# Gate loads from two queues, and seven sums ahead of the magnitudes on ScalarE

## The reference

```python
# x (64, 64, 1024), cond (64, 128); wk (8, 64, 64), bias_k (8, 64)
h = gelu(cond @ W0 + b0); h = gelu(h @ W1 + b1)
att = softmax(h @ W2 + b2)                       # (64, 8)
agg_w = einsum('bk,koi->boi', att, wk)           # a 64x64 matrix for each b
y = einsum('boi,bih->boh', agg_w, x) + (att @ bias_k)[:, :, None]

def bitlinear(x, w):                             # ternary weights
    scale = mean(abs(w))
    q = round(clip(w / (scale + 1e-5), -1, 1))
    return x @ (q * scale).T

out = x + bitlinear(bitlinear(y, w_gate) * bitlinear(y, w_up), w_down)
# w_gate, w_up (2752, 1024), w_down (1024, 2752)
```

## Time and profile before

| | us |
|---|---|
| median of 3 runs | 1855.11 (1854.92 to 1855.19) |
| the profiled execution | 1855.28, with a span of 1853.5 |
| busy: TensorE, VectorE, ScalarE, GpSimd | 1797.1, 955.6, 440.6, 132.6 |
| TensorE's first matmul starts | 6.18 |
| first convolution matmul starts | 25.56 |
| GpSimd's first scaling starts | 47.34 |
| second quantised tile starts | 62.96 |

### The profile page before, as it was taken

One profiled execution on the slowest core, in us unless ns is written; L12 is line 12 of the kernel. 1 busy time (PEld: TensorE's weight loads), 2 busy tenths in 40 slices (PEclk: granted clock), 3 DMA queues, 4 the chain that ended last, 5 costly groups with the idle time before them and its releaser, 6 DMA issues.

```text
span 1853.5 us, 29483 instructions
## 1 busy us (share of the span) xinstructions
PE 1797.1 (97%) x12151; PEld 1189.7 (64%) x12151; DVE 955.6 (52%) x1529; ACT 440.6 (24%) x712; POOL 132.6 (7%) x73
## 2 busy tenths in 40 slices
PE   5698999999999999999999999999999999999999
PEld 3344454444547895488846896488955888468854
DVE  5989961177533555245642556245652455435520
ACT  4667440112111222022211222112220222112110
POOL 0864500000000000000000000000000000000000
PEclk9799999999999999999999999999999999999999
DMA  8536410041101312022110321012120222012100
GB/s 298 171 127 247 131 52 29 32 165 70 66 29 50 108 51 77 29 100 67 61 56 32 115 70 66 29 53 106 51 77 30 106 77 73 30 38 80 51 18 29
DMA packets 47980, 145.74 MB, mean 79 GB/s; under 512 B 5552, under 2 KB 5872, under 8 KB 47856
## 3 DMA queue, kind: packets, MB, share of 16 engines
q1 hardware_dynamic: 47856, 143.88, 22.2%
HBM read 117.45 MB, written 26.41 MB: 78 GB/s over the span
## 4 chain that ended last, share of the span: by engine, by line
PE 91%; DVE 4%; ACT 2%; issue 2%; POOL 1%; DMA 0%; SPq 0%; DVEq 0%; ACTq 0%; POOLq 0%
PE ps L544 49%; PE ps L727 42%; DVE msk L1190 1%; ACT g_r L882 1%; POOL ys L516 1%; DVE msk L1182 1%; PE ps L626 0%; DVE aT L237 0%; ACT wgT L911 0%; POOL ab L527 0%; DVE wsum L1061 0%; DVE ys L1109 0%; ACT wuT L911 0%; DMA inter<-in_L_cond_b_dram 0%; POOL bbc L527 0%
## 5 line engine op out<-in xcount | busy, mean ns | idle before, releaser
L727 PE MATMUL ps<-yp,wgT 128*128 128x256 f16 x3528 | 773.4, 273 | 0.3 <-issue 0.2
L727 PE MATMUL ps<-wuT,wgT 128*128 128x256 f16 x3528 | 773.4, 273 | 0.0
L544 PE MATMUL ps<-wdT,inter 128*128 128x512 fp8e4 x2688 | 593.3, 379 | 0.0
L544 PEld LDWEIGHTS ps<-wdT,inter 128*128 128x128 f16 x2688 | 262.6, 98 | 314.4
L727 PEld LDWEIGHTS ps<-yp,wgT 128*128 128x128 fp8e4 x3528 | 345.3, 98 | 45.8 <-issue 5.4
L727 PEld LDWEIGHTS ps<-wuT,wgT 128*128 128x128 fp8e4 x3528 | 345.2, 98 | 40.8
L1240 DVE SCALAR_TENSOR_TENSOR xr<-ps,osc,xr 128x512 f32<-128x512 f32 x64 | 48.0, 750 | 406.0 <-PE ps L544 406.0
L544 PE MATMUL ps<-yp,wuT 128*128 128x512 f16 x672 | 152.9, 384 | 0.0
L544 PE MATMUL ps<-yp,wgT 128*128 128x512 f16 x672 | 150.5, 382 | 1.1 <-ACT wgT L911 1.1
L1001 ACT COPY raw<-ps 128x512 f32<-128x512 f32 (+1 forms) x66 | 37.3, 566 | 392.0 <-PE ps L727 392.0
L1425 DVE TENSOR_TENSOR wuT<-ps,msk 128x512 f32<-128x512 f32 (+1 forms) x66 | 44.0, 667 | 137.0 <-PE ps L727 136.2
(11 more groups left out here) (192 smaller groups left out, 1339.8 us busy)
## 6 DMA issues: line engine op xcount, KB each, us to landing
wgT<-wcomb SPq DMA_DIRECT2D x60, 896.0 KB, 4.8
xa<-in_x_dram SPq DMA_DIRECT2D x8, 2048.0 KB, 10.2
out_dram<-xr SPq DMA_DIRECT2D x64, 256.0 KB, 2.0
wdT<-in_L_ffn_w_up_dram SPq DMA_DIRECT2D x10, 512.0 KB, 4.3
wcomb<-raw SPq DMA_DIRECT2D x11, 448.0 KB, 2.5
ys<-in_L_ffn_w_down_dram SPq DMA_DIRECT2D x9, 512.0 KB, 4.0
wcomb<-msk SPq DMA_DIRECT2D x10, 448.0 KB, 2.4
xr<-in_L_ffn_w_down_dram SPq DMA_DIRECT2D x8, 512.0 KB, 4.5
```

The lines of the kernel that those rows point to most:

```text
L544: return nc.tensor.matmul(o, l, r, start=start, stop=stop)
L727: last = nc.tensor.matmul(out, w, operand(i, OPERAND[what])[:, k, :], start=(start and h + k + i == 0), stop=(k == KQ - 1 and i == 1), ski ...
```

## The change

Three edits. Gate loads with an odd number are no longer issued by SyncE but by ScalarE, all eleven ahead of its first Gelu. ScalarE's list has seven gate sums first, and then eight pairs of a magnitude and a sum, with the eight casts of y behind them. Gate tile 21 is summed by ScalarE and no longer by VectorE. SyncE's small inputs and x keep their place among the remaining gate loads.

```diff
-    SUM_DVE = (0, 1, 7, 10, 17, 21)
+    SUM_DVE = (0, 1, 7, 10, 17)
...
-                sp.dma_start(raw(e), tiles[n][0]).then_inc(s_raw[s], 16)
+                if e >= NG or e % 2 == 0:
+                    sp.dma_start(raw(e), tiles[n][0]).then_inc(s_raw[s], 16)
...
+            for e in range(1, NG, 2):
+                nc.scalar.dma_start(raw(e), tiles[loads[e][0]][0]).then_inc(s_raw[loads[e][3]], 16)
             act.wait_ge(s_pe, 2)
             nc.scalar.activation(h1, ps[1][:, 0:B], ACT.Gelu, bias=b0_sb).then_inc(s_ca, 1)
...
-            for k, n in enumerate((4, 5, 6, 8, 9, 11, 12, 13)):
+            for n in (4, 5, 6, 8, 9, 11, 12):
                 raw_sum(n)
+            for k, n in enumerate((13, 14, 15, 16, 18, 19, 20, 21)):
                 magnitudes(0, k)
-            for n, tiles_y in ((14, ()), (15, ()), (16, (0, 1)), (18, (2, 3)), (19, ()), (20, (4, 5, 6, 7))):
                 raw_sum(n)
-                for k in tiles_y:
-                    hi_y(0, k)
+            for k in range(KH):
+                hi_y(0, k)
             copy_T(0)
...
             for k in range(4):
                 split_y(0, k)
-            raw_sum(21)
             partition_sums(0, NG)
```

## The result

| | before | after |
|---|---|---|
| median of 5 runs, us | 1855.19 (1854.92 to 1856.83) | 1864.11 (1862.42 to 1864.83) |
| ratio | | 1.0044, 95% interval 1.0032 to 1.0055 |
| profiled execution, its span | 1855.28, 1853.5 | 1864.74, 1862.9 |

The changed kernel is 8.9 us slower. The forecast was 1861.9, range 1855.5 to 1867.

A forecast was written before the change was run, and what follows sets the result against it. The prediction took the first 60 us to be a chain of waits that TensorE depends on; +6.8 us for the conditioning weight and 0 for the rest gave 1862.1, less 0.17 for the median: 1861.9 us, range 1855.5 to 1867.

The forecast's parts named there:

- The main term: Conditioning weight, queues alternating packet by packet: lands at 22.0 us, aggregation needs it at 15.20, +6.8 us; chance 0.55.
- 418 GB/s: DMA drain rate assumed for the queued bytes, taken from large packets at 16 to 18 us.
- 20 ns each: Extra DMA engine time per small packet; 113 packets up to the conditioning weight make 2.3 us.
- the bias, x, the Gelu: Second-layer bias at 14.6 us, x at 27.0, Gelu possible at 8.1: each delay hidden behind other waits.
- Tile 12: Before the first magnitude: lands at 33.3 us, summed at 34.4, hidden by 0.8 us against 35.2.
- VectorE's sum: Removing VectorE's 1.20 us sum: threshold up to 1.2 us earlier, but value 0 since the chain runs through GpSimd.
- TensorE's clock: Shifted half-clock stretch at convolution or aggregation: minus 2 to up to plus 5 us.
- Rival 1: Small inputs slip through, but tile 12 delays the first magnitude: plus 5, 1860 us; chance 0.15.
- Rival 2: ScalarE's loads fill only what DMA engines leave free: net minus 1 to plus 2, 1855 us; chance 0.20.
- rival 3: Aggregation also at half clock, or ScalarE's full queue holds up SyncE's issues: 6.8 + 5, 1867 us; chance 0.10.

The follow-up runs named there:

- experiment 6: Changed kernel, but SyncE issues all small inputs ahead of gate tile 0; 1862.9 us, ratio 1.0039 to the kernel before.
- experiment 2: Kernel before with only the odd gate loads moved to ScalarE's queue, ScalarE's list and VectorE's sums as before; 1862.89 us, ratio 1.0043.
- experiments 3: Changed kernel, but ScalarE issues its eleven loads behind the Exp instead of ahead of the first Gelu; 1858.03 us, ratio 1.0015 to the kernel before.
- experiment 5: Kernel before with one edit: ScalarE issues the odd gate loads behind its Exp, old list kept; 1853.62 us, ratio 0.9989.
- experiment 8: Kernel before with SyncE's small inputs ahead of gate tile 0, SCD = 5, tile 21 summed by ScalarE, three sums before the first magnitude; 1851.25 us, ratio 0.9974.
- experiment 1: Changed kernel's ScalarE list and tile 21 sum on ScalarE, but all gate loads in SyncE's queue; 1857.25 us, ratio 1.0009 to the kernel before.

## Why the prediction was right

**The main term.** The forecast put +6.8 us on the conditioning weight, by packets taken in turn. The turns are in the trace (520 to 519), and the aggregation came 8.1 us later. The mechanism was right and the term 1.3 us too small. The gap is there from the start and doesn't grow: the first bias held TensorE until 10.67 instead of "about 9", the second layer's until 16.14 instead of 14.6, and the conditioning weight landed at 23.17 instead of 22.0. The sum let the queues drain at 418 GB/s from the first moment. The stretches view has the engines slower in the first three microseconds, and again from 12 to 14 us (the last two columns are their share and GB/s):

```profile
1.00:2.00 1.00, 0.00 (x0) 0.00 (x0) 0.00 (x0) 0.00 (x0) 0.94 (x6) 1.00 0.37 53
2.00:3.00 1.00, 0.00 (x0) 0.00 (x0) 0.00 (x0) 0.00 (x0) 0.49 (x2) 1.00 0.65 176
...
12.00:14.00 2.00, 0.01 (x1) 0.00 (x0) 0.00 (x0) 0.31 (x1) 0.00 (x0) 1.00 0.85 311
```
```profile
2.00:20.00 18.00, 2.44 (x9) 1.72 (x9) 1.39 (x8) 4.74 (x9) 0.49 (x2) 1.00 0.99 365
```

The 365 GB/s over 18 us are mostly no error of the sum: 6.57 MB at 418 and 1295 small packets over 16 engines at its 20 ns each are 15.7 + 1.6 = 17.3 us (an estimate by the forecast's own figures). The sum also left packets out. ScalarE's eleven loads made 1520 packets, where 84 for each engine are 1344: 16 more for each load. How the 1.3 us divide between the slow start and such packets no run shows.

What was last at the aggregation, and what was hidden behind it (the bias, x, the Gelu), was as forecast.

**The total.** 1861.9 was 2.2 us below the measured median. In the trace the scalings were 7.75 us late instead of 6.8, and 1.5 us were added at 183 us, at a place the forecast hadn't looked at. The mechanism carried the forecast; that these 1.5 us stayed inside the range is luck.

**Tile 12.** "Summed at 34.4, hidden by 0.8 us" failed. It counted the landing of tile 12 and one sum behind it. But tile 4 is the first of the seven and lands at 29.6; by then the tiles from ScalarE's queue had long landed and the others came faster than they could be summed, so seven sums ran end to end until 36.9. The bound was the landing of the first tile plus all seven sums, 2.5 us later than my figure. The forecast's own figures say it too: x at 27.0, tile 4 1.3 us behind it, and 7.4 us of sums make 35.7, past its 35.2 for the magnitude. It cost nothing in the changed kernel, where VectorE was waiting for TensorE, and 1.2 of the 2.2 us gained in experiment 6.

**VectorE's sum.** Value 0 was right, its first half was not. I wrote that the threshold would come up to 1.2 us sooner. It didn't come sooner at all relative to the scalings (63.74, against 55.99 before: +7.75). VectorE's next instruction waits for a cast, in its timeline:

```profile
60.60 0.16 DVE L1165 TENSOR_REDUCE tot<-wsum 128x1 f32<-128x22 f32 x1
62.48 1.09 DVE L1147 TENSOR_TENSOR yp<-ys,yp 128x512 f16<-128x512 f32 x1 [1.73 <-ACT yp L859]
```

The removed 1.2 us turned into waiting for tile 4 of ys, which GpSimd scales and ScalarE casts: 1.73 us instead of 0.40. On the rule of the Trainium skill (GPSIMD Engine Reference, section 8, Key points) that let the forecast leave this sum out, the trace agrees, as far as a sum with one input goes: all five scalings together took 11.27 us in both kernels.

**TensorE's clock.** The bound of -2 to +5 was put on the aggregation and the convolution. There little happened against before (8 matmuls in 6.01 us instead of 6.36, 16 in 3.76 instead of 3.75), since the half clock moved along with the convolution: it was 0.50 from 32 to 38 us. Against experiment 2, where the full clock came back sooner, it cost 0.8 us at the scalings. The 1.5 us came at 183 us. The bound on the size was wide enough, its place was wrong.

**The rivals.** Rival 1 (the head of the list alone) is what experiments 3 and 6 uncover, but not what set the time. Rival 2 (ScalarE's loads only fill gaps) fell: the engines filled up, and SyncE's small packets waited. Of rival 3, the aggregation at half clock didn't come (6.01 us for its 8 matmuls, at a granted clock of 1.00 from 24 to 30 us). SyncE's issues were held up, 7.02 us for x instead of 0.43, but x landed at 28.3 and the convolution started at 33.67, so that was hidden. On the rule of the Trainium skill (DMA: Bandwidth & Descriptors, section Queues, rings and completion order) that each DMA engine goes round robin a packet at a time: the trace agrees on the alternation. It differs on what a turn is: the page has some 9 to 17 descriptors in a typical packet, and here the turns are even when each contiguous piece is counted by itself.

## What to carry to other kernels

In these runs a second DMA queue was a second claim on the same engines, one packet for one packet. If the transfers that a chain waits for are many small pieces, bulk loads in another queue can cost them a full bulk packet per piece; issue the bulk behind them. Late in ScalarE's queue it was 1.9 us faster than before (experiment 5); all in SyncE's queue behind the small inputs it was part of experiment 8. And when a list of work is moved ahead of an instruction that others wait for, it ends with the latest of several sums: for each item, its landing plus the work from it to the end of the list. In the changed kernel the first item decided (29.6 us and seven sums), in experiment 1 the last (31.8 us and one sum).

## What the runs showed of the hardware

- The turns are exact to one packet in 500 (520 to 519, 502 to 503), and a 256-byte piece counts as much as a 4 KB one.
- ScalarE got 84 packets for each DMA engine out in 5.9 us at about 0.5 us an issue without being held. SyncE's issue of x, behind the conditioning weight's pieces, took 7.02 us:

```profile
8.13 7.02 SPq L397 DMA_DIRECT2D xa<-in_x_dram  x1
```

- From 20 to 22 us, when ScalarE's queue was running out (58 of its packets were left, against 720 of SyncE's), 733 of the 778 packets were under 512 bytes. They kept the engines full at 181 GB/s (share 1.22), less than half of the 418 that large packets gave before.
